# Eight of sixty-four tiles of slot logits computed inside attention, stored from ScalarE's queue and loaded back for dispatch

## The reference

```python
x = L0_attn_x                                   # (B=4, S=2048, D=256)
xn = layernorm(x)
# attention: 16 query heads, 4 key/value heads, head dim 16, causal
q = (xn @ wq.T).reshape(b, s, 4, 4, 16); k = (xn @ wk.T).reshape(b, s, 4, 16); v = ...
att = softmax(where(causal, -inf, einsum('bsgmd,btgd->bgmst', q, k) / 4))
ctx = einsum('bgmst,btgd->bsgmd', att, v).reshape(b, s, 256)
# soft mixture of 16 experts with 64 slots each
y = layernorm(xn, norm_g, norm_b); se = layernorm(slot_embeds, slot_g, slot_b) * scale
logits = einsum('bnd,esd->bnes', y, se)         # (4, 2048, 16*64 = 1024 slots)
dispatch = softmax(logits, axis=1)              # over the tokens
combine = softmax(logits.reshape(4, 2048, 1024), axis=-1)   # over the slots
slots = einsum('bnd,bnes->besd', y, dispatch)
gate = gelu(slots @ Wg + bg); up = slots @ Wu + bu; eout = (gate * up) @ Wd + bd
return x + ctx @ wo.T + einsum('bns,bso->bno', combine, eout)
```

## Time and profile before

| what | value |
|---|---|
| median of 3 runs | 2690.73 us (2684.36 to 2692.7) |
| the profiled execution | 2690.94 us, span 2689.2 us |
| mean granted TensorE clock | 0.981 |
| TensorE busy | 2580.5 us, 96% of the span |
| VectorE busy | 2046.0 us, 76% |
| ScalarE busy | 1728.3 us, 64% |
| GpSimd busy | 429.8 us, 16% |
| moved by DMA | 245.10 MB, mean 91 GB/s |

### The profile page before, as it was taken

One profiled execution on the slowest core, in us unless ns is written; L12 is line 12 of the kernel. 1 busy time (PEld: TensorE's weight loads), 2 busy tenths in 40 slices (PEclk: granted clock), 3 DMA queues, 4 the chain that ended last, 5 costly groups with the idle time before them and its releaser, 6 DMA issues. The chain is left out here.

```text
span 2689.2 us, 47797 instructions
## 1 busy us (share of the span) xinstructions
PE 2580.5 (96%) x16291; PEld 1541.4 (57%) x16291; DVE 2046.0 (76%) x4879; ACT 1728.3 (64%) x3510; POOL 429.8 (16%) x676
## 2 busy tenths in 40 slices
PE   7989999999999999999999999998989999999999
PEld 4444444444444444444444444367877888889999
DVE  8779989989999998998998898468475523356665
ACT  4577777778777777777777777867656651222221
POOL 6601111111111111111111111223130100100000
PEclk9968999999999999999999999999999999999999
DMA  7945423303312321330330000044333354545554
GB/s 255 309 116 64 54 34 45 45 11 42 45 21 30 45 33 17 45 45 6 45 45 6 8 8 29 9 174 173 125 130 145 102 187 141 172 155 194 194 192 150
DMA packets 175855, 245.10 MB, mean 91 GB/s; under 512 B 57205, under 2 KB 129017, under 8 KB 174105
## 3 DMA queue, kind: packets, MB, share of 16 engines
q1 hardware_dynamic: 160088, 227.73, 33.8%
q10 hardware_dynamic: 15552, 14.68, 1.8%
HBM read 156.21 MB, written 84.97 MB: 90 GB/s over the span
## 5 line engine op out<-in xcount | busy, mean ns | idle before, releaser
L809 ACT ACTIVATE att_pr<-att_ring 128x512 f32<-128x512 f32 (+3 forms) x2560 | 1174.3, 550 | 330.7 <-PE att_ring L890 323.8
L857 DVE TENSOR_REDUCE att_mx<-att_ring 128x1 f32<-128x512 f32 x1536 | 967.6, 680 | 75.5 <-PE att_ring L903 73.1
L903 PE MATMUL att_ring<-att_ks,att_qs 48*128 48x512 f32 (+3 forms) x1920 | 647.3, 422 | 16.3 <-ACT att_pr L809 6.8
L890 PE MATMUL att_ring<-att_qs,att_ks 64*128 64x512 f32 (+3 forms) x1920 | 576.3, 406 | 6.6 <-DVE att_mx L863 2.3
L890 PEld LDWEIGHTS att_ring<-att_qs,att_ks 64*128 64x128 f32 x1920 | 300.4, 186 | 401.8 <-DVE att_mx L857 145.2
L863 DVE CUSTOM_DVE_ANT_0 att_junk<-att_ring,w_causal 128x256 bf16<-128x256 f32 (+3 forms) x1024 | 466.1, 486 | 57.6 <-PE att_ring L903 31.2
L932 PE MATMUL att_acc<-att_pr,att_v 128*17 128x512 f32 (+3 forms) x3840 | 453.8, 544 | 2.7 <-ACT att_cT L820 1.5
L903 PEld LDWEIGHTS att_ring<-att_ks,att_qs 48*128 48x128 f32 x1920 | 307.1, 185 | 142.1 <-ACT att_pr L809 103.5
L760 POOL TENSOR_SCALAR_AFFINE_SELECT att_pr<-att_pr 128x512 f32<-128x512 f32 x256 | 162.5, 635 | 1031.4 <-ACT att_pr L809 1031.4
L903 PE MATMUL att_ring<-g_ks,g_qs 48*128 48x512 f32 (+3 forms) x640 | 227.7, 467 | 15.5 <-PEq L152 5.8
L1513 ACT CAST com_e1h<-com_tp 128x1024 fp32r<-128x1024 f32 x64 | 64.7, 1016 | 236.3 <-PE com_tp L1573 236.3
(11 more groups left out here) (170 smaller groups left out, 3271.1 us busy)
## 6 DMA issues: line engine op xcount, KB each, us to landing
slot_exps<-dis_e SPq DMA_DIRECT2D x64, 512.0 KB, 2.7
com_e<-slot_exps SPq DMA_DIRECT2D x64, 512.0 KB, 3.5
att_qs<-q_parts SPq DMA_DIRECT2D x72, 256.0 KB, 12.0
q_parts<-proj_part SPq DMA_DIRECT2D x32, 512.0 KB, 5.0
dis_y<-in_L_attn_x_dram SPq DMA_DIRECT2D x64, 256.0 KB, 2.8
att_ks<-k_parts SPq DMA_DIRECT2D x72, 128.0 KB, 12.7
y_cols<-proj_yT SPq DMA_DIRECT2D x16, 512.0 KB, 5.3
context<-att_cn SPq DMA_DIRECT2D x64, 128.0 KB, 2.0
```

The source lines that it names most:

```text
L809: nc.scalar.activation(pr[:, s % NPR, h, off:CH], spot(("s", s, h)), ACT.Exp, scale=float(HD) ** -0.5).then_inc(exp_done, 1)
L857: nc.vector.tensor_reduce(dst, spot(e), AX.X, ALU.max).then_inc(mb_used, 1)
L890: nc.tensor.matmul(spot(e), ks[g][r, kb * P:(kb + 1) * P], qs[g][r, c, hf * CH + off:(hf + 1) * CH], start=True, stop=True).then_inc(sT_re ...
L903: nc.tensor.matmul(spot(e), qs[g][r, c, q0:q0 + P], ks[g][r, j * CH:j * CH + wd], start=True, stop=True).then_inc(mb_ready, 1)
```

## The change

1. The logits of the first eight tiles of batch 0 (`NE = 8`) are computed in attention. Sixteen half tiles "l" (128 tokens by 512 slots, six matmuls) are put at the end of steps -17 to -2 of `program`, one per step, each in a bank of the ring. ScalarE copies a half tile from PSUM into the buffers of the exponentials, which are not in use yet, and stores it to DRAM ("first_logits") from its own queue. Before its first exponential (step 0) it waits for all sixteen stores.
2. For that, SP loads two chunks of y_cols when attention begins, and GpSimd splits them first of all.
3. The zero rows of groups 1 to 3 are no longer written by ScalarE. SP issues twelve DMAs that copy a row of zeros (`w["zero"]`, 256 columns) over 32 partitions each.
4. The queries of all four groups lie in one tile, whose place is the place of dispatch's logits of batch 0. In attention's last group SP loads the eight tiles back to their place there, once group 13 is through. (`part` of project lies in the same tile.)
5. In the steps without maxima, from 618 on, VectorE takes the row and column maxima of these eight tiles, three operations to two steps.
6. Phase L of batch 0 begins at tile 8. ScalarE's exponentials of both first batches are spread over the remaining 24 tiles, four to three tiles (`exps_by`), and SP's stores with them. The chunks of y_cols loaded ahead are 2, 3 and 4.

```diff
@@ project
+        room = queries[:, QW:]
+        part = room[:, 0:12 * CH].rearrange("p (q s h n) -> p q s h n", q=2, s=3, h=2)
-        part = a.sb("part", [P, 2, 3, 2, CH], F32R)
...
+                nc.gpsimd.memset(w["zero"][:].bitcast(F32), 0.0).then_inc(zeroed, 1)
@@ attend: program
+    NL = 2 * NE
+    L_FROM = -LEAD + 5
+        early = [("l", s - L_FROM)] if 0 <= s - L_FROM < NL else []
-        out = [st[0], xs[0], st[1], xs[1]] + ev + [xs[2], st[2], st[3], xs[3]] + av
+        out = [st[0], xs[0], st[1], xs[1]] + ev + [xs[2], st[2], st[3], xs[3]] + early + av
@@ attend: SP
+                for n in range(NEC):
+                    sp.dma_start(cols["low"][:, n].bitcast(F32), scr["yT_in"][0, n]).then_inc(cols["in"][n], 16)
+                for g in range(1, NKV):
+                    for rg in range(NRG):
+                        r = slice(RG * rg + 32, RG * (rg + 1))
+                        for dst, n in ((queries[r, g * QW:(g + 1) * QW], QW), (ks[g][r, :], S)):
+                            sp.dma_start(dst.bitcast(F32).rearrange("p (k n) -> p k n", n=D),
+                                         w["zero"][r, :].bitcast(F32).unsqueeze(1)
+                                         .to_broadcast([32, n // D, D])).then_inc(zeroed[g], 16)
...
+                    if s == STEPS - NU + AV_LAG:
+                        sp.wait_ge(l_out, 16 * NL)
+                        sp.wait_ge(pv_done, (NBG - 4 + -(-NE // 4)) * NU)
+                        for t in range(NE):
+                            sp.dma_start(lg[:, t, :], scr["first_logits"][t]).then_inc(l_in, 16)
@@ attend: GpSimd
+                for n in range(NEC):
+                    pool.wait_ge(cols["in"][n], 16)
+                    hi, lo = cols["high"][:, n], cols["low"][:, n]
+                    nc.gpsimd.tensor_copy(hi, lo.bitcast(F32)).then_inc(l_split, 1)
+                    pool.wait_ge(l_split, 2 * n + 1)
+                    nc.gpsimd.tensor_tensor(lo, lo.bitcast(F32), hi.bitcast(F32), ALU.subtract).then_inc(l_split, 1)
@@ attend: ScalarE
-                for g in range(1, NKV):
-                    for rg in range(NRG):
-                        r = slice(RG * rg + 32, RG * (rg + 1))
-                        zero = w["causal"][r, 0:1]
-                        nc.scalar.copy(qs[g][r].rearrange("p c n -> p (c n)"),
-                                       zero.to_broadcast([32, CPB * HL * CH])).then_inc(zeroed[g], 1)
-                        nc.scalar.copy(ks[g][r], zero.to_broadcast([32, S])).then_inc(zeroed[g], 1)
                 for s in ALL_STEPS:
+                    for e in program(s):
+                        if e[0] == "l":
+                            act.wait_ge(mb_ready, turn[e] + 1)
+                            nc.scalar.copy(half_tile(e[1]), spot(e)).then_inc(l_kept, 1)
+                            t, h = divmod(e[1], 2)
+                            act.wait_ge(l_kept, e[1] + 1)
+                            act.dma_start(scr["first_logits"][t, :, h * 512:(h + 1) * 512],
+                                          half_tile(e[1])).then_inc(l_out, 16)
+                    if s == 0:
+                        act.wait_ge(l_out, 16 * NL)
@@ attend: VectorE
+                def logit_maxes():
+                    dve.wait_ge(l_in, 16 * NE)
+                    for t in range(NE):
+                        nc.vector.tensor_reduce(nr[:, 0, t:t + 1], lg[:, t, :], AX.X, ALU.max, negate=True).then_inc(nr_ready, 1)
+                        yield
+                        ... (cm: a copy for t == 0, then a maximum)
+                        yield
                     if not maxes_of(s):
                         row_maxes(s - 1)
                         inverse_sums(s)
+                        next(side, None)
+                        if s % 2:
+                            next(side, None)
@@ attend: TensorE
+                        elif e[0] == "l":
+                            t, h = divmod(e[1], 2)
+                            wait_bank(pe, e)
+                            pe.wait_ge(l_split, 2 * (t // TPC) + 2)
+                            at, to = slice(t % TPC * P, (t % TPC + 1) * P), slice(h * 512, (h + 1) * 512)
+                            for k in range(DK):
+                                hi, lo = cols["high"][:, t // TPC, k, at], cols["low"][:, t // TPC, k, at]
+                                nc.tensor.matmul(spot(e), hi, seTh[:, k, to], start=(k == 0), stop=False)
+                                nc.tensor.matmul(spot(e), hi, seTl[:, k, to], start=False, stop=False)
+                                last = nc.tensor.matmul(spot(e), lo, seTh[:, k, to], start=False, stop=(k == DK - 1))
@@ dispatch
+        first_tile = lambda b: 0 if b else NE
+        SLOTS = 2 * TPB - NE
+        exps_by = lambda b, t: min(-(-2 * TPB * (b * TPB + t + 1 - NE) // SLOTS), b * TPB + t)
...
-                        for t in range(TPB):
+                        for t in range(first_tile(b), TPB):
...
-                            if t > 0:
-                                token_exp(b, t - 1)
+                            token_exps(exps_by(b, t) if b < 2 else b * TPB + t)
```

148 lines of the change are left out of this document (100 added, 48 removed).

## The result

The kernel with the change takes 2693.85 us (median of 12 runs, 2690.37 to 2699.18), beside 2688.84 us of the kernel before (12 runs, 2684.30 to 2692.73): ratio 1.002, interval 1.0012 to 1.0028. It is slower by about 5 us, where 13.4 us less were forecast. The profiled execution has a span of 2693.4 us, 4.2 us over that of before.

What follows compares the result with a forecast made beforehand. VectorE was taken to bound the head of attention, TensorE dispatch's first two phases. The terms -22.4 + 1.5 + 6 + 1.5 = -13.4 us gave 2677.5 us, own range 2668 to 2684, 8 in 10 within 2667 to 2700.

Steps and rivals of the forecast that it cites:

- The lead to the first score: Head of attention: half tiles and remaining fills on TensorE against VectorE's maxima, with clock rise and small waits; plus 6 us.
- the other terms: Head of attention: 1.1 us TensorE over VectorE, 1 us waiting for GpSimd's transpose, 1 us for hiccups.
- The zeros: Head of attention: 4.7 MB on SP's queue, some 25 us, through by 191 and hidden by the maxima; no cost.
- The wait for all sixteen stores: Before ScalarE's first exponential in attention: the last store lands slightly late; plus 1.5 us, bounds 0 and 8.
- the queues hold the head: Rival, head of attention: slow zeros or late logit stores delay the first exponential 6 to 9 us; 2685.5 us, 11%.
- What ScalarE and the two buffers give back: Dispatch's first two phases: small waits for exponential buffers and the burst of normalisations; plus 1.5 us, bounds 0 and 20.
- The sign that the prediction gave: Dispatch's first two phases: 20 to 22 us shorter, TensorE busy 10.00 of 10.00 us until the burst of normalisations.
- The tail: End of attention: the last cast of row maxima some 1 us late, nearly 3 us of cover; costed at nothing.
- The removed matmuls: Dispatch's first phase: eight tiles leave, 96 matmuls at 0.233 us each; 22.4 us less TensorE time.
- the exponentials: Rival, dispatch's first two phases: exponentials become the bound when stores land later, some 8 us more; 2685.5 us, 10%.

Runs made afterwards that it cites:

- p: Kernel before, with only ScalarE's twelve zero fills replaced by twelve SP DMAs of zeros over 32 partitions; 2687.75 us, ratio 0.9998.
- e: Changed kernel, but GpSimd writes the zero rows behind the first and second row maxima and SP's twelve zero DMAs are gone; 2697.03 us, ratio 1.0027.
- d: Changed kernel with its single wait, but loads of the second and third groups moved later, to steps 6 and 22; 2689.60 us, ratio 1.0000.
- a: Changed kernel, but in dispatch's first two phases SP issues stores of exponentials before the next load of columns; 2687.29 us, ratio 0.9996.
- q: f, plus three exponentials before dispatch's first copy and loads of columns issued from ScalarE's queue; 2676.74 us, ratio 0.9951.
- f: Changed kernel with SP's stores before loads, a wait per buffer at the first four steps, and later group loads; 2681.09 us, ratio 0.9959.
- r: q, but the second phase's burst of eight normalisations is spread over four tiles, two at a time; 2673.59 us, ratio 0.9943.
- l: f, but ScalarE takes three exponentials before dispatch's first copy, the other 29 spread over the 24 tiles; 2675.73 us, ratio 0.9944.
- b: Changed kernel, but ScalarE waits at steps 0 to 3 only for the four stores out of the buffer it then writes; 2686.09 us, ratio 0.9995.
- o: a, but ScalarE issues the loads of columns from its own queue, behind the copy they waited for; 2691.88 us, ratio 1.0007.

## Why the prediction was wrong

The direction was wrong: 2677.5 forecast, 2693.85 measured. Two terms of the sum failed, each put at 1.5 us: the wait for all sixteen stores cost 11.1 us, and what ScalarE and its two buffers give back was 12.2. By its own steps:

- **The lead to the first score**, forecast +6: measured +5.0. VectorE and TensorE were even, as reckoned; the first half tile stood at 167.24 with its columns split in time; the clock rose 7.9 us after it (6 assumed, which costs 1 us more), and the other terms came to 2 us less than their 3.1. Right as a sum; that these two misses partly cancel is luck.
- **The zeros**, forecast 25 us, through by 191, free: the last was issued at 179.26, the median one landed after 9 us and all by 188.6, 30 us after the first was issued (the middle of the 17 and 41 us given is 29, not 25). p shows that they cost nothing, and e that the late stores were not theirs. Right.
- **The wait for all sixteen stores**, forecast +1.5 with bounds 0 and 8: measured +11.1 (11.92 us from first score to first exponential, 0.80 before), of which 2.5 came back up to the first cT, in part because of the clock: between the first exponential and the first cT it was at 0.50 for 11.3 us before and for 8.0 us in the changed kernel. This is the step that failed. The prediction named the loads of the second group and their share of 0.98, and then priced a store by how it lands beside other things. By d and e a store lands in 2.0 us without these loads and in 13.1 us beside them. The upper bound, "a store that waits its turn at every packet", was a number without a row: the row that bears on it, 21 us at 0.98 moving 114 GB/s, says that the engines are full until the loads are through, and the loads end when they end. The rival "the queues hold the head" had the mechanism (2685.5 us), with 6 to 9 us and a chance of 11%. Of the two reasons that it gave, the loads were the one, and the zeros had no part in it.
- **What ScalarE and the two buffers give back**, forecast 1.5 with bounds 0 and 20: measured 12.2 (phases -10.2 for -22.4). 5.1 of it is the order on SP's queue (a), which no step of the prediction looked at. It asked how long a store takes to land, not what stands ahead of it: every fourth tile SP waits for the next tile's logits, issues a load of 512 KB, and only then comes to the stores. Before, the exponential was taken behind the next tile's copy and so was never ready earlier than the load; now it is. In a, TensorE's idle time is still 4.2 us and its half-clock loss 1.9 us over those of before; these are most of the remaining 7 us. I put the idle time down to two buffers that each come free about 4 us after use, and to the burst. A part of it q recovers; that the rest is the buffers was not shown by itself, since no run has a third one. The sign that the prediction gave, 10.00 of 10.00 us until the burst, did not come: TensorE stood idle for 2.13 and 2.05 us ahead of it.
- **The tail**, forecast 0 for 1 us of delay with 3 us of cover: 0.3 us late. Right.
- **The removed matmuls**, 22.4 us: 77.1 us would be the phases with the losses of before and no others, and q comes to 80.90. Without idle time and half-clock loss the phases are 90.3 us before and 68.8 in the changed kernel, 21.5 less. The size was right.

The sum again: -13.4 + 9.6 + 10.7 (the two misses) - 2.5 (came back) - 1.0 (lead) + 0.9 (the other stages) = +4.3, against +4.2 in the profiled executions. The two missed terms are those of two rivals, the queues and the exponentials, each priced at 8 us more and 2685.5 us. The prediction took them one at a time; both came, and 2677.5 + 8 + 8 would have been 2693.5.

The edits of f undo most of both, and then the change is worth 0.4% (2681.09), with those of q and r 0.5 to 0.6%, near what was forecast.

## What to carry to other kernels

A wait that guards a reused buffer should ask for the stores of that buffer alone; asked for everything, it inherits the slowest transfer of a busy moment, and that moment is found by asking which loads are in flight when the last stores are issued (here they were issued 8 to 13 us ahead of the last one). Moving those loads gave more than the finer wait, 9.2 against 5.3 us, and with them moved the finer wait gave nothing. On a queue, what frees a buffer goes ahead of what has to wait for another engine: when work is moved between engines, read again what each queue's next instruction waits for, also where the diff hasn't touched that queue's order. Taking 32 us off an engine that nobody waits for (p) moves nothing.

## What the runs showed of the hardware

- **One stream, two clocks.** The same instructions see the clock rise at two moments. In the second half tile the changed kernel is at the low clock (0.79 us for its first matmul) and gets the high one in the third; d has it in the second already:

```profile
171.76 0.79 PE L978 MATMUL att_ring<-w_seTh,w_yTh 128*128 128x512 f32 x1
...
175.65 0.40 PE L979 MATMUL att_ring<-w_seTl,w_yTh 128*128 128x512 f32 x1
```
```profile
167.88 0.51 PE L978 MATMUL att_ring<-w_seTh,w_yTh 128*128 128x512 f32 x1
```

  The first half tile began at 167.24 and at 163.71: the clock rose 7.9 to 9.0 us after it in the changed kernel, f, l and q (first score after 48.2 to 48.7 us) and 3.2 to 4.1 us after it in a, b, d, e, o and r (46.3 to 46.6). That is 2 us of the head by chance.
- **A busy TensorE at half its clock.** In b it is busy 5.00 of 5.00 us at 0.50 from 220 to 225, on six matmuls of 48 rows, six of 64 and sixteen products with V. The Trainium skill, "TensorE: Matmul & The Clock Gate" (Part 1: The HAM clock gate), gives a busy engine its full clock; the trace disagrees here as it did before the change.
- **A DMA issue can hold its queue.** In p, from the third on, each of the twelve DMAs of zeros held SP for 1.1 to 2.7 us where the two before took 0.7, from 158.72 to 179.1, while the DMA engines moved 192 GB/s at a share of 0.95. The first row maxima went out right behind them, 8 us later after the start of attention than before, and the first score came no later for it (43.28 us, 43.27 before).
